# Second buffers for weight sums and activation parts, and a new order for the next batches' layer norms, in a cross-attention block on one core

## What is computed

```python
x = layer_norm(hidden, ln1_w, ln1_b)
q = x @ q_w + q_b;  k = ctx @ k_w + k_b;  v = ctx @ v_w + v_b      # 16 heads of 32
attn = softmax(q k^T / sqrt(32) + mask)
hidden = attn v @ cproj_w + cproj_b + residual
y = gelu(layer_norm(hidden, ln2_w, ln2_b) @ fc_w + fc_b)           # 512 -> 2048
out = hidden + y @ proj_w + proj_b                                 # 2048 -> 512
```

## Time and profile before

| | |
|---|---|
| median of 3 runs | 834.61 us (833.38 to 835.18) |
| profiled execution, device time | 833.2 us |
| its span | 831.4 us |
| PE busy | 747.7 us, 90% of the span |
| DVE busy | 546.7 us, 66% |
| POOL busy | 448.3 us, 54% |
| ACT busy | 362.2 us, 44% |
| mean granted clock of PE | 0.969 |

### The profile page before, as it was taken

How to read it: one execution, slowest core, us unless ns; L and a number is a source line. 1 busy time by engine, 2 the same in 40 slices (tenths; PEclk the granted TensorE clock), 3 DMA queues, 4 the chain that set the end, 5 groups by cost and what they waited for, 6 DMA issues and landing times.

```text
span 831.4 us, 10419 instructions
## 1 busy us (share of the span) xinstructions
PE 747.7 (90%) x3568; PEld 505.1 (61%) x3568; DVE 546.7 (66%) x1077; ACT 362.2 (44%) x618; POOL 448.3 (54%) x307
## 2 busy tenths in 40 slices
PE   7999999989999999999995888987775988899998
PEld 5888876433443434444483667765554866678776
DVE  6764357788888898887846556468675236554564
ACT  4433332576665666767724344212123433432221
POOL 2724040479987887886437623534844234235673
PEclk9999999999999999999997999989977989999999
DMA  8657295867567747886173215253822512133442
GB/s 304 229 165 278 98 283 158 254 178 183 138 161 193 218 130 189 195 176 229 29 184 105 76 51 190 76 110 116 246 86 77 164 51 76 52 89 92 143 129 79
DMA packets 118196, 124.24 MB, mean 149 GB/s; under 512 B 41248, under 2 KB 66084, under 8 KB 118144
## 3 DMA queue, kind: packets, MB, share of 16 engines
q1 hardware_dynamic: 118000, 123.56, 51.8%
q10 hardware_dynamic: 144, 0.02, 0.0%
HBM read 94.05 MB, written 29.37 MB: 148 GB/s over the span
## 4 chain that ended last, share of the span: by engine, by line
PE 67%; DVE 19%; issue 4%; POOL 4%; ACT 3%; DMA 2%; SPq 2%; ACTq 0%; DVEq 0%
PE ps L588 18%; PE ps L590 17%; PE ps L589 17%; DVE ps L1278 5%; PE ps L711 4%; PE ps L695 4%; PE ps L680 3%; PE ps L726 3%; DVE BIG L1322 2%; DVE R L1481 2%; DVE R L1214 1%; POOL BIG L1595 1%; DVE HR L1391 1%; SPq L410 1%; DVE BF L1381 1%
## 5 line engine op out<-in xcount | busy, mean ns | idle before, releaser
L956 ACT ACTIVATE Pt<-ps 128x512 f32<-128x512 f32 x256 | 137.7, 598 | 71.9 <-PE ps L695 70.5
L1595 POOL TENSOR_TENSOR BIG<-RW,BIG 128x512 fp32r<-128x512 f32 x66 | 101.5, 1542 | 112.7 <-ACT BIG L1057 110.9
L588 PE MATMUL ps<-BIG,HR 128*128 128x512 f32 x256 | 105.7, 413 | 31.5 <-DVE HR L1393 28.8
L1057 ACT ACTIVATE BIG<-RW 128x512 fp32r<-128x512 f32 x64 | 40.2, 631 | 154.8 <-PE ps L590 135.1
L590 PE MATMUL ps<-BIG,HR 128*128 128x512 f32 x256 | 103.5, 404 | 0.0
L589 PE MATMUL ps<-BIG,HR 128*128 128x512 f32 x256 | 103.3, 404 | 0.0
L695 PE MATMUL ps<-BIG 98*128 98x512 f32 x256 | 93.3, 440 | 4.2 <-ACT Pt L956 3.7
L1278 DVE CUSTOM_DVE_ANT_0 ps<-ps,FU 128x512 f32<-128x512 f32 x128 | 84.6, 723 | 15.4 <-PE ps L680 15.3
L1278 DVE CUSTOM_DVE_ANT_0 ps<-ps,BIG 128x512 f32<-128x512 f32 x128 | 84.6, 724 | 10.9 <-PE ps L680 10.8
L695 PEld LDWEIGHTS ps<-BIG 98*128 98x128 f32 x256 | 44.1, 187 | 68.8 <-issue 29.6
L588 PEld LDWEIGHTS ps<-BIG,HR 128*128 128x128 f32 x256 | 50.6, 198 | 47.4 <-DVE HR L1393 33.4
(11 more groups left out here) (160 smaller groups left out, 1607.5 us busy)
## 6 DMA issues: line engine op xcount, KB each, us to landing
RW<-in_proj_w SPq DMA_DIRECT2D x64, 256.0 KB, 2.7
BIG<-qs SPq DMA_DIRECT2D x62, 256.0 KB, 2.9
BIG<-ks SPq DMA_DIRECT2D x62, 256.0 KB, 3.2
RW<-in_fc_w SPq DMA_DIRECT2D x48, 256.0 KB, 3.1
ks<-BIG SPq DMA_DIRECT2D x32, 256.0 KB, 2.0
qs<-BIG SPq DMA_DIRECT2D x32, 256.0 KB, 6.0
R<-hd SPq DMA_DIRECT2D x20, 256.0 KB, 3.9
R<-in_x SPq DMA_DIRECT2D x16, 256.0 KB, 5.5
```

Source lines behind the costliest of these rows:

```text
L588: eng.matmul(outp, a[0], b[0], start=first, stop=False, skip_group_check=onto)
L956: eng.activation(Pt[:, r, j % 2, :], bank(bank_a(("s2", i, j))), ACT.Exp, scale=SCALE).then_inc(S["a_ra"], 1)
L1057: eng.activation(second(n)[0], raw_w(at), ACT.Copy).then_inc(S["a_pj"], 1)
L1595: eng.tensor_tensor(dst, src, high.bitcast(F32), ALU.subtract).then_inc(S[name], 1)
```

## The change

1. `SUMS` becomes two tiles, `FU` and the first half of the memory under `R0`/`RX`; `weight_sums(m)` waits for `rest_low` of m - 2, and `rest_low(p + 2)` moves ahead of `add_c12(p)` on DVE; `rest_low(1)` moves ahead of `add_u2(0)`.
2. Activation parts get a third place (`RX[:, 1024:2048]`). The front weights that used `RX` go to `RY` (over `R1`) and `BIG`.
3. `RAW_W` has the two slices of the rest's p = 0 after the sixth front slice instead of after the eighth; the slots' order follows, and the loads of p = 1's slices now wait for `rest_low(0)`.
4. In the front of q = 0 norms and transposes of batch 1 come before the last division of attention, the transposes 2 and 3 use `R0`, and the differences and their parts are spread over p = 4 to 6.
5. In the second product of q = 0 the layer norms of batches 2 and 3 are laid out one or two operations to each n; `add_out`, `y_high`, `y_low` and the differences are spread, and `block_low` of batches 2 and 3 moves into the front of q = 1. `bias_add` of the second batch of a pair moves from n = 21 to n = 28.

```diff
-        SUMS = FU.rearrange("p a n -> p (a n)")
+        SUMS = [t.rearrange("p a n -> p (a n)") for t in (FU, R0[:, 0:2, :])]
+        def parts_of(n):
+            return HR[:, n % 3] if n % 3 < 2 else RX[:, 1024:2048].rearrange("p (h t) -> p h t", h=2)
+        def turned(b, c):
+            return R0[:, c % 2, :] if b == 1 and c >= 2 else FU[:, c % 2, :]
         for q in range(2):
-            RAW_W += [("wf", HF * q + p, p) for p in range(HF)]
             for p in range(HF):
+                RAW_W += [("wf", HF * q + p, p)]
+                if p == 5:
+                    RAW_W += [("wr", HF * q, 0), ("wr", HF * q, HF)]
+            for p in range(1, HF):
                 RAW_W += [("wr", HF * q + p, p), ("wr", HF * q + p, p + HF)]
...
             # SPq, p loop
+                    if q == 0 and p < 6:
+                        load_raw_w(first + p + 6)
+                    if q == 0 and p < 2:
+                        y_store(1, 2 * p)
+                        y_store(1, 2 * p + 1)
                     if q == 0 and p == 1:
-                        y_store(1, 0)
-                        y_store(1, 1)
-                    if q == 0 and p == 2:
-                        y_store(1, 2)
-                        y_store(1, 3)
                         y_load(1)
...
             # POOL, weight_sums
-                if m:
-                    pool.wait_ge("v_wr", 2 * m)
+                if m >= 2:
+                    pool.wait_ge("v_wr", 2 * m - 2)
...
             # DVE, split_hidden
-                    dve.wait_ge("p_pr", 4 * (n - 1))
+                elif n >= 3:
+                    dve.wait_ge("p_pr", 4 * (n - 2))
...
             # DVE, the rest
                 rest_low(q, 0)
+                rest_low(q, 1)
                 add_u2(q, 0)
-                rest_low(q, 1)
                 add_u3(q, 0)
                 add_c22(q, 0)
                 for p in range(HF):
                     if p + 1 < HF:
                         add_u2(q, p + 1)
                     add_c21(q, p)
-                    add_c12(q, p)
                     if p + 2 < HF:
                         rest_low(q, p + 2)
+                    add_c12(q, p)
...
             # DVE, second product
-                    if n == 17:
-                        add_out(2 * q)
+                    if 21 <= n < 23:
+                        add_out(2 * q, (2 * n - 42, 2 * n - 41))
                     if q == 0:
+                        for b, at in ((2, 10), (3, 15)):
+                            if 0 <= n - at < 2:
+                                for c in (2 * (n - at), 2 * (n - at) + 1):
                                     norm(LN[b], b % 2, 4 + b, c)
+                        for b, at in ((2, 12), (3, 16)):
+                            if 0 <= n - at < 4:
+                                y_block(b, n - at)
+                        for b, at in ((2, 19), (3, 23)):
+                            if 0 <= n - at < 2:
+                                for k in (2 * (n - at), 2 * (n - at) + 1):
                                     y_affine(b, k)
-                        if n == 25:
-                            blocks(1)
+                        if 25 <= n < 29:
+                            block(1, n - 25)
                         if 28 <= n:
                             front_low_part(1, n - 28)
...
             # POOL, second product
-                    if n == 21:
+                    if n == 28:
                         bias_add(2 * q + 1)
-                        if n == 17:
-                            for k in range(4):
-                                y_low(2, k)
+                        if 21 <= n < 23:
+                            y_low(2, 2 * n - 42)
+                            y_low(2, 2 * n - 41)
```

More of the change, by code:

```diff
@@ L46, in cross_attention_block @@
         RX = sb("RX", [128, 2048], R)
-        R1 = sb("R1", [128, 4, 512], F32)
+        with nc.sbuf_tensor("R1", [128, 4, 512], F32) as R1:
+            pass
+        RY = sb("RY", [128, 2048], R)
         R2 = sb("R2", [128, 4, 512], F32)
@@ L790, in fc_rest @@
                     pe.wait_ge("v_c22", m + 1)
-                product(outp, [x[:, 256 * a:256 * a + 256] for x in rest(p)], YQ[y], (0, 1),
+                product(outp, [x[:, 256 * a:256 * a + 256] for x in rest(q, p)], YQ[y], (0, 1),
                         which in (6, 5)).then_inc(S[done], 1)
@@ L1159, in _ @@
                         split_out(NS - 1)
-                    if q == 0 and p == 6:
-                        for n in range(4):
+                    if q == 0 and p == 4:
+                        block_high(0, 0)
+                        block_high(0, 1)
+                    if q == 0 and p == 5:
+                        for n in (2, 3, 4):
                             block_high(0, n)
-                    if p == 6 and q:
+                    if p == 6:
                         rest_high(q, 0)
-                if q == 0:
-                    block_high(0, 4)
-                    rest_high(q, 0)
                 rest_high(q, 1)
@@ L1507, in _ @@
                     if q and p == 0:
-                        add_out(1)
-                    if q == 0 and p + 2 < HF:
-                        front_low_part(0, p + 2)
+                        add_out(1, range(4))
+                    if q and p < 3:
+                        block_low(1, p)
                     if q and p >= 4:
@@ L1513, in _ @@
                     if q == 0 and p == 0:
+                        front_low_part(0, 2)
+                        for c in range(4):
+                            norm(LN[1], 1, 5, c)
+                        y_block(1, 0)
+                        y_block(1, 1)
                         divide_a(NS - 1)
@@ L1517, in _ @@
                         divide_c(NS - 1)
-                        for c in range(4):
-                            norm(LN[1], 1, 5, c)
                     if q == 0 and p == 1:
-                        y_block(1, 0)
-                        y_block(1, 1)
-                    if q == 0 and p == 2:
                         y_block(1, 2)
                         y_block(1, 3)
+                        front_low_part(0, 3)
+                    if q == 0 and 2 <= p < 6:
+                        front_low_part(0, p + 2)
                     if q == 0 and 3 <= p < 7:
@@ L1530, in _ @@
                         eng.tensor_tensor(R2[:, c, :], bank(c), R2[:, c, :], ALU.add).then_inc(S["v_cp"], 1)
-                    if q == 0 and p == 4:
+                    if q == 0 and p == 3:
                         for k in range(4):
                             y_affine(1, k)
+                    if q == 0 and p == 4:
+                        block(0, 0)
+                        block(0, 1)
                     if q == 0 and p == 5:
-                        blocks(0)
+                        block(0, 2)
+                        block(0, 3)
                     if q == 0 and p == 6:
-                        block_low(0, 0)
-                        block_low(0, 1)
+                        for n in range(3):
+                            block_low(0, n)
                 rest_low(q, 0)
+                rest_low(q, 1)
                 add_u2(q, 0)
-                rest_low(q, 1)
                 add_u3(q, 0)
@@ L1575, in _ @@
[L1575 to L1584 removed]
+                        if n == 11:
+                            for c in range(4):
+                                aggregate(1, 7, c)
+                            variances(1, 7)
@@ L1585, in _ @@
+                        if 25 <= n < 29:
+                            block(1, n - 25)
                         if 28 <= n:
                             front_low_part(1, n - 28)
-            add_out(3)
+            add_out(3, range(4))
         @block.gpsimd
@@ L1740, in _ @@
                     root(0, 4)
+            root(1, 5)
             out_low(NS - 2)
-            root(1, 5)
             x_add(3, 0)
@@ L1750, in _ @@
             for q in range(2):
+                if q:
+                    for n in (3, 4):
+                        block_low(1, n)
                 weight_sums(q, 0)
+                weight_sums(q, 1)
                 if q == 0:
-                    for n in (2, 3, 4):
+                    for n in (3, 4):
                         block_low(0, n)
-                else:
-                    bias_add(2)
                 for p in range(HF):
-                    if p + 1 < HF:
-                        weight_sums(q, p + 1)
-                    if q == 0 and p == 2:
-                        bias_add(0)
-                    if p == HF - 1:
-                        for n in range(3):
-                            second_low(32 * q + n)
+                    if p + 2 < HF:
+                        weight_sums(q, p + 2)
+                    if p == 3:
+                        bias_add(2 * q)
+                for n in range(3):
+                    second_low(32 * q + n)
                 for n in range(32):
```

138 lines of the change are left out of this document (66 added, 72 removed).

## The result

The changed kernel took 806.37 us (median of 4 executions, 804.81 to 807.62) beside 834.0 us of the kernel before on the same chip: ratio 0.967, 95% interval [0.9644, 0.9696]. It is faster, as forecast, but 14 us above the forecast 792.4 and 2.4 us above the range's upper end. Its profiled execution took 805.86 us (span 804.0), 27.3 us less than the one before. One execution of experiment e14 ran throughout at a granted clock of 0.56 (1197.57 us); it is left out of e14's ratio, and e14's stages are read from e15, a second run of the same kernel.

A forecast was written before the change was run, and what follows sets the result against it. PE was taken as the engine that could set the time, held up by waits. Gains of 6.6 + 31.0 + 1.9 + 2.7 = 42.2 us from the median 834.61 gave 792.4 us, range 783 to 804.

The forecast's parts named there:

- the second product of q = 0, gain 31.0: Feed-forward's second product, first q: a third place removes most PE waits for DVE; 98.7 instead of 129.65 us.
- (b): End of q = 0's second product: DVE's and ACT's front parts for q = 1 delay split 29; 8.5 us.
- (a): q = 0's second product, n = 24 to 26: a transpose awaits SPq's stores, then POOL's paired y_low; 3 us.
- Front and rest of q = 0, gain 6.6: First front and rest: gapless steps, less a late front slice and a wait for weights; ends 511.4, not 518.05.
- the chain to 7(0): Start of q = 0's rest: loads, sums, ACT and DVE from rest_low(0)'s end to PE's block product 7(0); 11.5 us.
- The rests' steps: Both rests: rest_low no longer waits for add_c12, so steps take 6.8 us with no gap but the last.
- The start of the first rest, and q = 1: Shared slots delay p = 1's weights at each rest's start; front and rest of q = 1 gain only 1.9 us.
- (1): Rival: the third place's lead goes unused, half the old waits in q = 0's second product stay; 803 us, chance 0.17.
- my own sign of failure: q = 0's second product: PE waiting for L1393 in the middle, n = 10 to 20, would show the prediction wrong.
- (2): Rival: POOL's sums collide with rest_low, pushing it past 6.8 us in every rest step; 802 us, chance 0.09.
- (3): Rival: front slice 6 arrives in time and the turn to q = 1 is half as dear; 784 us, chance 0.08.
- (4): Rival: the four weight slots serialise the rests, each step taking 11.5 us instead of 6.8; 858 us, chance 0.03.

The follow-up runs named there:

- e14: Changed kernel with POOL's four y_low of batch 2 subtracting only 16 of 512 columns; ratio 0.9639 to the kernel before.
- e13: Changed kernel with POOL's second_low for n = 3 to 31 subtracting only 16 of 512 columns; ratio 0.9585 to the kernel before.
- e4: Changed kernel with only two places for the activation parts, layer norms still in the new layout; ratio 0.9773 to the kernel before.
- e2: Changed kernel with q = 1's four front_low_part put behind the last split on DVE; ratio 0.9627 to the kernel before.
- e15: Second run of e14's kernel (changed kernel, y_low of batch 2 cut to 16 of 512 columns), for its trace; second product of q = 0 took 106.05 us.
- e1: Changed kernel with transposes 2 and 3 of batch 3 put in the free first half of RX; ratio 0.9681 to the kernel before.
- e10: Kernel before with one edit, rest_low(p + 2) ahead of add_c12(p) on DVE; ratio 0.9806 to the kernel before.
- e6: Changed kernel with one tile for the weight sums instead of two; ratio 0.971 to the kernel before.
- e3: Changed kernel with the weight slices loaded in their old order, all front slices before the rest's first; ratio 0.9483 to the kernel before.

## Why the prediction was wrong in size

**The failed step: the second product of q = 0, gain 31.0.** It measured 18.9, outside its bounds of 20 and 40. The step rested on the sentence that all 86.08 us of DVE's busy time, collisions included, fit into 87.2. The sum of a kernel in which DVE waits for PE is not that of one in which it doesn't: with most of the waits gone the same work took 98.71 us. I took the collisions as a fixed part of the old busy time, though they depend on who starts first, and the change moves just that (8 casts behind a POOL operation became 16). e13 bounds their size from above: without `second_low`, and so without the old collisions with it too, the stage takes 100.1 us, 1.4 above the 98.7 forecast. The step also gave the credit to the wrong part: it began with the third place and its lead of two `pj`, and e4 shows that without that place 16.7 of the 18.9 us are still gained.

The remaining waits were found in part in the right places. (b), the turn, was forecast at 8.5 us; its two gaps are 6.99 + 1.47 us, and moving its cause away takes 10.7 from this stage and gives 6.1 to the next (e2). (a) was forecast at 3 us for a store and `y_low` together, at n = 24 to 26: `y_low` alone is worth 4.6 (e15), and the store's wait came at `pj(20)` and is worth 1.2 (e1). These prices overlap: 10.6 (e13) + 10.7 + 4.6 + 1.2 make 27.1, and the stage stands only 23.5 above PE's 87.2.

The Trainium skill (SBUF — State Buffer, "Who interferes with whom") says that the issue order decides which of DVE and GpSimd blocks. Here the trace agrees in both directions: POOL's 1.60 and 1.29 us, the cast's 0.43 and 1.45. I had used this rule for the rests' sums, where it changed little, and for splits beside runs of POOL operations, but not for each split beside `second_low`, where the change turned the order round.

**Stores.** The claim that each wait at n = 10 to 20 comes out under 3 us, with 2.0 us for a store, was too low: DVE waited 4.66 us for a store whose four issues took 2.29 us and stood behind a reload and a weight load. PE felt 4.27 of it, but removing it gave 1.2 (e1).

**Front and rest of q = 0, gain 6.6.** Measured 4.3, at its lower bound, and 3.7 without the 0.6 from before the stage. PE reaches the first block product of the rest at 445.1 (forecast 445.0). ACT did stand at a front slice behind the reload, until 428.14 where the forecast had the slice land at 427.9. But PE's stalls were split the other way round (ACT, then PE):

```profile
428.14 0.63 ACT L1043 ACTIVATE RY<-RW 128x512 fp32r<-128x512 f32 x1 [8.29 <-DMA RW<-in_fc_w]
...
414.82 0.47 PE L600 MATMUL ps<-YT,BIG 128*128 128x512 f32 x1 [2.93 <-DVE BIG L1328]
...
429.31 0.50 PE L600 MATMUL ps<-YT,BIG 128*128 128x512 f32 x1 [0.39 <-ACT BF L999]
```

`front_low` behind the transposes, forecast at 0.4 us, cost 2.93, and the slice, forecast at 2.8, only the 0.39 that were left of its delay. The slice still set the time, so the sum of 3.3 for 3.2 came out; that the first part was so much too low did no harm by luck. Then the chain to 7(0) took 1.5 us more than 11.5 (457.98 - 445.0), mostly for one operation that met POOL's `block_low` (DVE, POOL):

```profile
454.96 2.26 DVE L1337 TENSOR_TENSOR BIG<-R,BIG 128x1024 fp32r<-128x1024 f32 x1 [3.18 <-ACT BIG L1060]
...
453.80 5.64 POOL L1624 TENSOR_TENSOR YT<-BF,YT 128x1024 fp32r<-128x1024 f32 x2
```

1.22 without it. The rest then took 55.7 us instead of the forecast 54.9.

**The rests' steps** were right: 6.8 us and no gap but the last. The reason was right as to the order on DVE (e10, e6), and the second tile for the sums played no part.

**The start of the first rest, and q = 1:** 7(0) of q = 1 comes 33.8 us after the front's start (658.15 - 624.36) where 33.6 was forecast (681.3 - 647.7), and the gain is 1.4 for 1.9. That the price of the slots eats what the gaps gave is shown by e3. I had costed it as a term of each stage, but not seen that undoing this one part would give 15 us.

**The rivals.** (1), 803 us, is nearest in number, and it is right in part: e4 shows that the want of a place was not what made DVE late, as two places with the new layout lose only 2.2 us. But most of the old waits did not stay, and no PE wait over 0.5 us stands before n = 20, in e4 only one of 0.61. The longer DVE time left too little of the lead to cover the store's wait; my own sign of failure, a wait in the middle, came as the 4.27 us at n = 20. (2) was right that collisions decide and wrong about the place. (3) and (4) did not happen. (The chances of the five cases add up to 1.00 before the 0.01 that I left for no change.)

What stays open: how much of the third place's 5 to 8 us (e4) comes from outside the stage, where only 2.2 show, and how much of e13's 10.6 us belongs to the collisions that the change added and how much to those that were there before.

## What to carry to other kernels

An engine's busy time with its waits is no floor for its busy time without them: before costing a deeper buffer, ask which two engines the old wait kept apart, and add the collisions that its removal makes. Try a change of order alone first: here two moved lines in the kernel before gave 16.5 us where the whole change gave 27, the second tile nothing, and the reordered loads cost 15. A wait's length in the trace is not its price: 4.27 us were worth 1.2, and 8.5 at the turn were worth 10.7 in their own stage but 4.6 with the next one, where the work went.

## What the runs showed of the hardware

A DVE cast of 128x512 that starts 0.13 us behind a POOL operation of 1.29 us takes 1.45 us instead of 0.43, and over 31 of them the mean rose from 0.63 to 0.95 us. The block difference L1350 of 128x1024 took 2.32 us when it started 0.41 us behind a POOL operation, and 1.22 when POOL's started 0.66 us behind it; POOL's then took 1.71 instead of 1.29. The transposes kept their 0.70 us also where a POOL operation had started first. `statistics` kept its 0.69 where a POOL operation started 0.5 us into it (changed kernel) and where one had started 0.37 us before it (e13).
